# Norms of the last tail on 256 tokens, with block 1's between the halves of block 0 and its end norm, sum and store in two halves

## What is computed

```python
x = L0_attn_input_tensor                          # (8, 1024, 256)
# layer 1: projections, causal convolution, a state-space scan over the tokens,
# a norm over each head for the whole sequence, a gate, and the product with Wout
x = x + _layernorm(_L0_attn_ref(_layernorm(x, axis=-1), ...), axis=-1)
# layer 2: 256 -> 1024 with binarised weights, gelu, 1024 -> 256 with binarised weights
x = x + _layernorm(_L0_ffn_ref(_layernorm(x, axis=-1), ...), axis=-1)

def _layernorm(x, axis=-1, eps=1e-05):
    m = jnp.mean(x, axis=axis, keepdims=True)
    v = jnp.var(x, axis=axis, keepdims=True)
    return (x - m) / jnp.sqrt(v + eps)
```

## Time and profile before

| | us |
|---|---|
| median of 3 runs (1370.19 to 1372.21) | 1371.21 |
| the profiled execution: its own time | 1372.45 |
| the profiled execution: its span | 1370.7 |
| PE busy in it (94%) | 1286.9 |
| DVE busy in it (74%) | 1008.7 |
| ACT busy in it (54%) | 746.8 |
| POOL busy in it (36%) | 491.5 |

### The profile page before, as it was taken

The page is one execution under the profiler, slowest core; times in us unless marked ns, Lnnn a source line. Parts: engine busy times, 40 slices in busy tenths (PEclk is TensorE's granted clock), DMA queues, the critical chain, the costliest instruction groups (busy, mean ns, idle before and its releaser), DMA issues.

```text
span 1370.7 us, 27653 instructions
## 1 busy us (share of the span) xinstructions
PE 1286.9 (94%) x10552; PEld 812.6 (59%) x10552; DVE 1008.7 (74%) x2364; ACT 746.8 (54%) x1270; POOL 491.5 (36%) x551
## 2 busy tenths in 40 slices
PE   6998999999999999999999999999999999999675
PEld 3564647565575756656575655757556565666543
DVE  5565786869777696877868688686968768685575
ACT  5564664647655485554745567454855547455321
POOL 2030435134441543224442344414443254332533
PEclk9899999999999999999999999999999999999888
DMA  7010000101010010101001010000101000010100
GB/s 220 1 48 16 2 0 2 47 1 48 0 48 1 3 46 1 48 1 47 1 1 47 2 47 1 23 26 1 47 1 48 1 30 3 1 33 1 32 1 31
DMA packets 30563, 32.88 MB, mean 24 GB/s; under 512 B 1856, under 2 KB 28628, under 8 KB 30432
## 3 DMA queue, kind: packets, MB, share of 16 engines
q1 hardware_dynamic: 30432, 31.11, 7.2%
HBM read 22.72 MB, written 8.39 MB: 23 GB/s over the span
## 4 chain that ended last, share of the span: by engine, by line
PE 40%; DVE 25%; issue 16%; POOL 13%; ACT 6%; POOLq 0%; DVEq 0%; ACTq 0%
PE bank L1383 22%; PE bank L1558 5%; POOL Cd L774 4%; DVE xs L1046 4%; PE bank L1543 4%; POOL y L739 3%; DVE hh L1241 2%; DVE un L1021 2%; POOL xdw L769 2%; PE bank L1525 2%; POOL state L785 2%; DVE gn_stats L1165 1%; DVE sh L1051 1%; ACT L950 1%; DVE uh L1230 1%
## 5 line engine op out<-in xcount | busy, mean ns | idle before, releaser
L1383 PE MATMUL bank<-sh,WbT 128*128 128x512 f16 x768 | 177.2, 387 | 10.6 <-DVE sh L1051 10.6
L1383 PE MATMUL bank<-sh,WcT 128*128 128x512 f16 x768 | 175.9, 379 | 0.0
L960 ACT ACTIVATE mt<-bank 128x512 f32<-128x512 f32 x128 | 69.5, 597 | 186.7 <-PE bank L1465 186.7
L1046 DVE SCALAR_TENSOR_TENSOR xs<-xi,vectors,xs 128x512 f32<-128x512 f32 x192 | 152.5, 804 | 7.5 <-ACT xs L876 3.2
L769 POOL TENSOR_TENSOR xdw<-xdt,decays 128x512 f32<-128x512 f32 x64 | 66.7, 1042 | 236.8 <-DVE xdt L1133 236.8
L1383 PEld LDWEIGHTS bank<-sh,WbT 128*128 128x128 f16 x768 | 74.2, 99 | 101.8 <-issue 15.3
L1558 PE MATMUL bank<-uh,sign1T 128*128 128x512 f16 x512 | 122.8, 386 | 7.5 <-DVE uh L1230 7.2
L1543 PE MATMUL bank<-WoutT,yT 128*128 128x256 f32 x512 | 117.4, 386 | 12.6 <-POOL yT L753 6.5
L1383 PEld LDWEIGHTS bank<-sh,WcT 128*128 128x128 f16 x768 | 75.2, 98 | 86.5
L988 ACT ACTIVATE hf<-bank,vectors,alpha 128x512 f32<-128x512 f32 x128 | 99.5, 777 | 45.8 <-PE bank L1558 33.6
L1571 PE MATMUL bank<-sign2T,hh 128*128 128x256 f16 x1024 | 119.3, 275 | 1.8 <-DVE hh L1241 1.8
(11 more groups left out here) (186 smaller groups left out, 2539.5 us busy)
## 6 DMA issues: line engine op xcount, KB each, us to landing
xt<-L_attn_input_tensor_dram SPq DMA_DIRECT2D x16, 512.0 KB, 5.0
u<-L_attn_input_tensor_dram SPq DMA_DIRECT2D x16, 512.0 KB, 4.0
out_dram<-u SPq DMA_DIRECT2D x16, 512.0 KB, 2.9
yT<-in_L_ffn_w_dram SPq DMA_DIRECT2D x2, 512.0 KB, 9.6
u<-in_L_ffn_w_dram SPq DMA_DIRECT2D x2, 512.0 KB, 8.9
BT<-in_L_attn_Wx_dram SPq DMA_DIRECT2D x1, 512.0 KB, 4.7
BT<-in_L_attn_Wz_dram SPq DMA_DIRECT2D x1, 512.0 KB, 5.6
zs<-in_L_attn_Wb_dram SPq DMA_DIRECT2D x1, 512.0 KB, 5.5
```

Source lines behind the costliest of these rows:

```text
L960: nc.scalar.activation(mt[n % 2][:, g].rearrange("p c t -> p (c t)"), bank(t, ("seg", j, q, g))[:, :], ACT.Exp).then_inc(seg_exp.sem, 1)
L1046: nc.vector.scalar_tensor_tensor(out=xs[:, c, :], in0=xi[:, c, k:k + BLK], scalar=taps[:, c, k:k + 1], in1=xs[:, c, :], op0=ALU.mult, op1= ...
L1383: mm = nc.tensor.matmul(bank(t, key)[:, :], w[i][:, k, cols(m)], v[h][:, k, :], start=(a == 0), stop=(a == len(terms) - 1))
```

## The change

It changes the order in `last_tail` and the size of the pieces there. The statistics, roots, norms and sums of `mid` and `ff` each work on 256 tokens (two tiles, m = 0 or 1) in place of 512. The steps of block 1 are put between those of block 0, in part between the hidden steps of block 0. The norm's output of block 1 goes to `xt[1]`, which is free by then, and no longer to `un`. The statistics of `end` in block 0 move from behind the last hidden split of block 1 to behind its second one. In block 1 the last scale, bias, statistics and roots go by 256 tokens, its norm and sum have a step for each half, and its store is two DMAs of 256 tokens. The semaphores of the norms count halves. The instructions of the other tails stay as they are.

```diff
@@ last_tail @@
-    steps += [("Wo", 0, 0), ("Wo", 0, 1), ("mid_stat", 0), ("mid_norm", 0), ("ff_stat", 0), ("ff_norm", 0)]
...
+    steps += [("Wo", 0, 0), ("mid_stat", 0, 0), ("Wo", 0, 1), ("mid_norm", 0, 0), ("mid_stat", 0, 1)]
...
+    steps += [*hidden(1, 0, 2), ("end_stat", 0), ("end_root", 0), *hidden(1, 2, 8), ("end_norm", 0), ("end_add", 0)]
+    for m in range(2):
+        steps += [("O", 1, m), ("end_stat", 1, m), ("end_root", 1, m)]
+        steps += [("end_norm", 1, 0), ("end_add", 1, 0)] if m else []
+    steps += [("end_norm", 1, 1), ("end_add", 1, 1)]
@@ new helpers @@
+        def tiles(m):
+
+            return range(NQ) if m is None else range(2 * m, 2 * m + 2)
+
+        def mid_buffer(t, j):
+
+            return xt[j] if isinstance(t.b, int) and (t.b + t.d, j) == (NB - 1, NJ - 1) else un
@@ block.sync @@
-            for j in range(NJ):
-                store(Batch(NB - 1), j)
...
+            store(t, 0)
+            for m in range(2):
+                sp.wait_ge(*o_out.count(t, (NJ - 1) * NQ + 2 * m + 2))
+                sp.dma_start(rows(out_v, t, NJ - 1)[:, 2 * m:2 * m + 2, :], u[NJ - 1][:, 2 * m:2 * m + 2, :])\
+                    .then_inc(stored[NJ - 1].sem, 16)
@@ inverse_root, POOL @@
-                    pool.wait_ge(*ln_eps[w].count(t, j + 1))
-                    pool.tensor_tensor(rstd[w][:, :], var_eps[w][:, :], power[:, 0:NQ], ALU.pow)\
-                        .then_inc(ln_rstd[w].sem, 1)
+                    at = tiles(m)
+                    pool.wait_ge(*ln_eps[w].count(t, (j * NQ + at.stop) // 2))
+                    pool.tensor_tensor(rstd[w][:, at.start:at.stop], var_eps[w][:, at.start:at.stop],
+                                       power[:, 0:len(at)], ALU.pow).then_inc(ln_rstd[w].sem, len(at) // 2)
@@ statistics, DVE @@
-                for i in range(NQ):
+                at = tiles(m)
+                for i in at:
                     ready(i)
                     nc.vector.bn_stats(stats[w][:, i, :], tile(i)).then_inc(ln_stats[w].sem, 1)
@@ middle_norm, DVE @@
+                v = mid_buffer(t, j)
+                if v is un:
+                    s, sj = before_block(t, j)
+                    dve.wait_ge(*full(s, ("uT", sj, KD - 1)))
+                for i in tiles(m):
+                    normal("mid", t, j, v[:, i, :], attention_tile(t, j, i), i, m).then_inc(mid_out.sem, 1)
```

More of the change, by code:

```diff
@@ L739, in add_bias, with add_middle @@
                 pool.tensor_tensor(v, v, b2_row[:, None, :].to_broadcast([P, 2, D]), ALU.add).then_inc(y2_out.sem, 1)
-            def add_middle(t, j):
-                for i in range(NQ):
+            def add_middle(t, j, m=None):
+                for i in tiles(m):
                     pool.wait_ge(*y2_norm.count(t, j * NQ + i + 1))
@@ L1002, in _, with statistics, normal @@
                 s.prime(dve)
-            def statistics(w, t, j, tile, ready):
-                for i in range(NQ):
+            def statistics(w, t, j, tile, ready, m=None):
+                at = tiles(m)
+                for i in at:
                     ready(i)
                     nc.vector.bn_stats(stats[w][:, i, :], tile(i)).then_inc(ln_stats[w].sem, 1)
-                dve.wait_ge(*ln_stats[w].count(t, (j + 1) * NQ))
+                dve.wait_ge(*ln_stats[w].count(t, j * NQ + at.stop))
                 dve.sem_inc(stats_seen, 1)
-                for i in range(NQ):
+                for i in at:
                     nc.vector.bn_aggr(moments[w][:, i, :], stats[w][:, i, :]).then_inc(ln_moments[w].sem, 1)
-                dve.wait_ge(*ln_moments[w].count(t, (j + 1) * NQ))
-                dve.wait_ge(*ln_rstd[w].count(t, j))
-                nc.vector.tensor_scalar(var_eps[w][:, :], moments[w][:, :, 1], EPS, None, ALU.add)\
-                    .then_inc(ln_eps[w].sem, 1)
-            def normal(w, t, j, dst, src, i):
-                if i == 0:
-                    dve.wait_ge(*ln_rstd[w].count(t, j + 1))
+                dve.wait_ge(*ln_moments[w].count(t, j * NQ + at.stop))
+                dve.wait_ge(*ln_rstd[w].count(t, (j * NQ + at.start) // 2))
+                nc.vector.tensor_scalar(var_eps[w][:, at.start:at.stop], moments[w][:, at.start:at.stop, 1], EPS, None, ALU.add)\
+                    .then_inc(ln_eps[w].sem, len(at) // 2)
+            def normal(w, t, j, dst, src, i, m=None):
+                at = tiles(m)
+                if i == at.start:
+                    dve.wait_ge(*ln_rstd[w].count(t, (j * NQ + at.stop) // 2))
                 return nc.vector.tensor_scalar(dst, src, moments[w][:, i, 0:1], rstd[w][:, i:i + 1],
@@ L1206, in attention_tile, with middle_stats, middle_norm, ff_stats @@
                 return bank(t, ("Wo", j, i // 2))[:, (i % 2) * D:(i % 2 + 1) * D]
-            def middle_stats(t, j):
+            def middle_stats(t, j, m=None):
                 statistics("mid", t, j, lambda i: attention_tile(t, j, i),
-                           lambda i: dve.wait_ge(*full(t, ("Wo", j, i // 2))))
-            def middle_norm(t, j):
-                s, sj = before_block(t, j)
-                dve.wait_ge(*full(s, ("uT", sj, KD - 1)))
-                for i in range(NQ):
-                    normal("mid", t, j, un[:, i, :], attention_tile(t, j, i), i).then_inc(mid_out.sem, 1)
-            def ff_stats(t, j):
+                           lambda i: dve.wait_ge(*full(t, ("Wo", j, i // 2))), m)
+            def middle_norm(t, j, m=None):
+                v = mid_buffer(t, j)
+                if v is un:
+                    s, sj = before_block(t, j)
+                    dve.wait_ge(*full(s, ("uT", sj, KD - 1)))
+                for i in tiles(m):
+                    normal("mid", t, j, v[:, i, :], attention_tile(t, j, i), i, m).then_inc(mid_out.sem, 1)
+            def ff_stats(t, j, m=None):
                 statistics("ff", t, j, lambda i: u[j][:, i, :],
-                           lambda i: dve.wait_ge(*u_out.count(t, j * NQ + i + 1)))
-            def ff_norm(t, j):
-                for i in range(NQ):
-                    normal("ff", t, j, un[:, i, :], u[j][:, i, :], i).then_inc(un_out.sem, 1)
+                           lambda i: dve.wait_ge(*u_out.count(t, j * NQ + i + 1)), m)
+            def ff_norm(t, j, m=None):
+                for i in tiles(m):
+                    normal("ff", t, j, mid_buffer(t, j)[:, i, :], u[j][:, i, :], i, m).then_inc(un_out.sem, 1)
             def middle_low(t, j):
@@ L1252, in ffn_out, with end_stats, end_norm @@
                     .then_inc(y2_scaled.sem, 1)
-            def end_stats(t, j):
+            def end_stats(t, j, m=None):
                 statistics("end", t, j, lambda i: ffn_buffer(t, j)[:, i, :],
-                           lambda i: dve.wait_ge(*y2_out.count(t, j * NQ // 2 + i // 2 + 1)))
-            def end_norm(t, j):
-                for i in range(NQ):
+                           lambda i: dve.wait_ge(*y2_out.count(t, j * NQ // 2 + i // 2 + 1)), m)
+            def end_norm(t, j, m=None):
+                for i in tiles(m):
                     v = ffn_buffer(t, j)[:, i, :]
-                    normal("end", t, j, v, v, i).then_inc(y2_norm.sem, 1)
+                    normal("end", t, j, v, v, i, m).then_inc(y2_norm.sem, 1)
             def weights(t, name, k):
```

24 lines of the change are left out of this document (13 added, 11 removed).

## The result

The changed kernel takes 1374.14 us (median of 10 runs, 1373.28 to 1375.74). The kernel before takes 1371.05 (10 runs beside it, 1369.61 to 1372.87). The ratio is 1.0023, with an interval from 1.0013 to 1.0032: about 3.1 us slower. I had said 1370.9, with a range up to 1373.8.

The account below looks back on a forecast made before the run. PE bounds the whole kernel; in the tail DVE, POOL and PE take turns. Against 1371.2, +0.27 to the last sum and -0.75 for the store gave 1370.7; the number given was 1370.9, range 1368.9 to 1373.8.

Parts of the forecast that it names:

- The change leaves that part alone, however. Only the last tail changes: Whole kernel ahead of the last 80 us: PE-bound and untouched by the change, so no cost was counted there.
- a hold-up elsewhere: A hold-up not seen in the prediction, no place or size given; chance 0.05.
- The hidden steps: Head of the tail, block 0: PE starts them 0.55 us earlier; nothing with roots of 1.02, 0.9 with 0.51.
- The output of block 0: Output matmuls after block 0's hidden steps: PE's pause of 3.63 us stays, and they are done 0.25 us earlier.
- the head's gain: Head of the tail: PE starts 0.55 us earlier, half then lost to the clock, leaving 0.25 us.
- The first fall of the clock: Block 0's hidden steps: clock at 1.2 GHz from about 1315.8, down for some 5.4 us of the dense matmuls.
- The last split: Block 1's hidden steps: it ends at 1353.9, against 1352.10, with 2.05 us of statistics now ahead of six splits.
- rival 1: Block 1: the clock falls near 1353 and is back at 1357.5; +0.6 us in all, 1371.8; chance 0.20.
- my sum: Last tail: +0.27 to the last sum, -0.75 for the halved store, -0.5 us together, giving 1370.7.
- The store: End of the span: the last store halved to 256 KB saves 0.75 us, leaving 2.7 behind the last sum.
- the forecast's own range: Whole kernel: 1369.9 us with two-column roots of 0.51 to 1371.6 with roots of 1.02.
- Rival 4: Whole tail: gains and losses cancel more closely than could be counted, 1371.2; chance 0.45 together with the forecast.

Follow-up runs that it names:

- e1: The kernel before with only the norm semaphores between DVE's epsilon step and POOL's root counting in twos, old tail order; 1374.95 us, ratio 1.0027.
- e5: The kernel before with increments by two on DVE's epsilon step alone, POOL's root counting by ones; 1375.55 us, ratio 1.0034.
- e6: The kernel before with increments by two on POOL's root alone; 1371.07 us, ratio 1.0001.
- e7: The kernel before, increments by one, with a long-fulfilled third wait added so the epsilon step's own wait stands apart; 1374.48 us, ratio 1.0027.
- e2: The changed kernel with every increment one, the tail's halves counting on semaphores of their own; 1370.62 us, ratio 0.9996 to the kernel before.
- e10: The changed kernel with increments of one and another end: late block 0 statistics, first half summed before the second root; 1369.94 us, ratio 0.9989.

## Why the prediction was wrong

**The step that failed** is "The change leaves that part alone, however. Only the last tail changes": all but the last 80 us was costed at nothing, on the ground that the instructions of the other tails stay as they are. That ground holds for the order but not for the instructions. The runs put +2.8 us of turns in its place (changed, e1), all but 0.4 of it from DVE's epsilon step (e5, e6), by a wait that stands apart (e7). All my rivals were in the tail, and for a hold-up elsewhere I left 0.05. The Trainium skill (Trainium Kernel Development and Optimization, Key Constraints) says that compute semaphores must increment "by 1". Two works here, but e1 measures what it costs: 1.0027. The Trainium skill (Perfetto Trace Analysis, Identifying Dependency Chains) says that instructions that wait for several engines may get instructions ahead of them for the further waits. The trace agrees: in e7 the third wait puts the epsilon step 0.06 us later.

**The tail** came out at +0.45 us where I had -0.5, and at -0.1 with increments by one (e2). So about 0.5 of the miss is again the increments (on the old tail e1 has +0.6), and 0.4 is the order itself. Point by point, counted from the start of the gates, before against changed:

- A root on two columns took 0.70 to 0.72 us, and 0.80 beside a DVE operation. I had 0.8, between bounds of 0.51 and 1.02, so it was 0.1 too high.
- The hidden steps start 0.57 us earlier (21.56 against 22.13). I had 0.55. The sum was right by errors that cancel: the roots were faster than 0.8, and the last `ff` norm of block 0 took 1.53 us beside a POOL sum, not 0.7.
- DVE's pause was 2.86 us (nearly 3), PE's pause 3.37 (over 3), and the clock fell behind it. The output of block 0 starts 0.36 us earlier, not 0.55: DVE worked for 11.57 us behind the first gelu where it was 11.36 before, since the second split took 1.5 us beside POOL's sum and not the 1.07 of my count. It ends 0.05 us later than before, and I had it 0.25 earlier: with the clock down, its 64 matmuls took 9.34 us and not 8.93. In e2 and e10 the output starts no earlier than before at all (37.38 us behind the gates' start). So the head's gain was a term that I had too high.
- The first fall of the clock lasted only until 1320.6, 2.9 us into the dense hidden steps, where I had some 5.4. In e2 and e10 it lasted as long as before. No run shows why, so it can't be put down to the change.
- The last split ends 2.1 us later (1.8 said). In e2 it is 1.9; the rest is the increments.
- The clock fell once more, at about 1354.7, and came back 3.4 us later. This is rival 1, to which I gave 0.20, and it is the term that put the end above my sum. The matmuls end 3.6 us later than before, where I had 1.7. It acts through the first output bank, not the second as I wrote: the first scale waits 1.55 us for PE. In e2, which has the fall without the increments, the first bias starts 0.8 us later than in my sum and the second 0.85. The last root comes back cheaper than I said (0.80 beside a norm, where I had 0.8 and 0.3 more), so the end is 0.4 above my sum, where the rival had 1.1.
- The store: from the end of the last sum to the end of the span it is 2.6 us, against 3.4. I had 2.7: right.

So if the increments had been ones, the time of e2, 1370.62, would have been within the forecast's own range. That would have been luck in part: the clock fell in block 1, which the forecast left out, and the head gave 0.1 where I had 0.25; both errors were small enough for the range. Rival 4, that gains and losses cancel, describes the reordering best.

## What to carry to other kernels

When a change makes a helper count in other units, look at what each instruction outside the changed place now carries. An increment or a third wait can cost an instruction its own wait, and in a chain of short dependent steps on one engine that is 0.06 us each time, 2.3 us over this kernel. The reverse is where the gain was: an instruction in such a chain that only counts cost more (0.11 us a norm) than all the reordering of the last tail gave. And where PE's clock in the first batch makes executions differ by 2 us, compare the distance between two events of each trace, not the spans.

## What was not expected of the hardware

- An instruction of DVE that increments a semaphore by two has its wait ahead of it in another instruction, and starts 93 ns behind the end of the operation that it waits for; with an increment of one it is 34 ns. Increments by two on POOL put the start of a root 314 ns behind the start of the epsilon step, against 249.
- Of raising to a power on POOL, four columns take 1.02 us and two take 0.71. An estimate from these two is 0.15 us a column on top of some 0.4. Beside a split of DVE, four took 1.51 when they started 0.02 us behind it, and 1.01 when they started 0.09 ahead.
- An epsilon step on two columns took 0.75 us, not 0.17, beside POOL's last gate multiply, and a split of 0.69 took 1.10 beside POOL's sum in the changed kernel.
- PE's clock fell although PE was never idle for more than 0.67 us at a time, with two matmuls in every 1.07 us. In the kernel before, a stretch of the same kind but half as long left it at 1.00.
